# A fused attention-and-experts layer on one core: other orders of VectorE's and ScalarE's work per token tile

## The reference

```
x = L0_attn_x                                    # (2, 1024, 512) float32
sa, ca, ga, sb, cb, gb = the six parts of silu(c) @ wmod, per batch
h = layernorm(x) * (1 + ca) + sa
x = x + ga * mixer(h)
h = layernorm(x) * (1 + cb) + sb
x = x + gb * ffn(h)

mixer(h):  x_shift = (roll(h, -512) @ Wts.T) * g + h * (1 - g)
           xn = layernorm(x_shift) * ln_w + ln_b
           k, v = xn @ Wk.T, xn @ Wv.T
           wkv = exp(-exp(time_first) * sigmoid(k)) * v
           states = scan over the tokens: s = s * exp(time_decay) + wkv
           out = states @ Wo.T
ffn(h):    router softmax, the best 4 of 32 experts, at most 64 tokens per expert
           shared = silu(h @ Wsg) * (h @ Wsu) @ Wsd, times sigmoid(h @ Wse)
           each expert: silu(xe @ Wg) * (xe @ Wu) @ Wd, weighted, added to its tokens
```

## Time and profile before

| | us |
|---|---|
| median of 3 runs | 717.41 |
| lowest and highest run | 716.9, 723.52 |
| the profiled execution | 721.89 |
| its span | 720.1 |
| PE busy in the span | 675.2 (94%) |
| DVE, ACT, POOL busy | 365.6, 288.5, 184.7 |

### The profile page before, as it was taken

One profiled execution on the slowest core, in us unless ns is written; L12 is line 12 of the kernel. 1 busy time (PEld: TensorE's weight loads), 2 busy tenths in 40 slices (PEclk: granted clock), 3 DMA queues, 4 the chain that ended last, 5 costly groups with the idle time before them and its releaser, 6 DMA issues.

```text
span 720.1 us, 8883 instructions
## 1 busy us (share of the span) xinstructions
PE 675.2 (94%) x3218; PEld 470.2 (65%) x3218; DVE 365.6 (51%) x702; ACT 288.5 (40%) x552; POOL 184.7 (26%) x174
## 2 busy tenths in 40 slices
PE   4899699999998899998999899999999999999997
PEld 3666466777666667886665566666665666668875
DVE  3778677678688877763214223122121233225755
ACT  3435775565747623323225224233132343323231
POOL 1254474745536200001122022222221122120000
PEclk9789887999999999999999999999999999999999
DMA  7760200000241008107667767878899788816311
GB/s 272 269 216 0 76 15 30 15 30 30 74 145 60 15 1 313 53 1 268 239 237 237 256 218 248 265 237 282 271 317 325 242 270 266 285 21 235 115 50 70
DMA packets 50295, 118.27 MB, mean 164 GB/s; under 512 B 6904, under 2 KB 11084, under 8 KB 50252
## 3 DMA queue, kind: packets, MB, share of 16 engines
q1 hardware_dynamic: 45388, 109.31, 43.2%
q0 software_dynamic: 4864, 8.40, 5.4%
HBM read 100.87 MB, written 18.91 MB: 166 GB/s over the span
## 4 chain that ended last, share of the span: by engine, by line
PE 60%; DVE 6%; DMA 3%; ACT 3%; issue 2%; POOL 2%; SPq 0%; DVEq 0%; ACTq 0%; POOLq 0%
PE bank L1688 26%; PE bank L1700 11%; PE bank L1743 11%; PE bank L1760 6%; DMA egu<-in_L_ffn_Wu_dram 2%; PE bank L1731 1%; ACT xsH L863 1%; DMA xg<-h_rows,slot_tok 1%; PE bank L1791 1%; PE bank L1749 1%; DVE xres L1262 1%; POOL ho L637 1%; DVE prodL L1226 1%; DVE prod L1224 1%; POOL rsh L609 1%
## 5 line engine op out<-in xcount | busy, mean ns | idle before, releaser
L1688 PE MATMUL bank<-xsH,wguH 128*128 128x512 f32 x352 | 143.1, 406 | 1.1 <-DVE xsL L1216 0.7
L1688 PE MATMUL bank<-xsL,wguH 128*128 128x512 f32 x352 | 137.5, 391 | 0.0
L1688 PE MATMUL bank<-xsH,wguL 128*128 128x512 f32 x352 | 137.3, 390 | 0.0
L1743 PE MATMUL bank<-egu,xeT 128*64 128x352 f32 x512 | 81.0, 470 | 4.5 <-DMA egu<-in_L_ffn_Wu_dram 3.2
L1688 PEld LDWEIGHTS bank<-xsH,wguH 128*128 128x128 f32 x352 | 66.3, 188 | 25.0 <-issue 10.5
L1224 DVE TENSOR_TENSOR prod<-bank,silu 128x512 f32<-128x512 f32 x38 | 26.2, 690 | 110.3 <-PE bank L1688 87.7
L1700 PE MATMUL bank<-wdH,prodH 128*128 128x512 f32 x176 | 74.1, 421 | 6.3 <-DVE prodL L1226 4.2
L695 POOL DMA_INDIRECT expert_sums<-ye,slot_to x32 | 48.7, 1522 | 118.0 <-DMA expert_sums<-ye,slot_to 91.4
L1688 PEld LDWEIGHTS bank<-xsL,wguH 128*128 128x128 f32 x352 | 66.1, 188 | 14.6
L1688 PEld LDWEIGHTS bank<-xsH,wguL 128*128 128x128 f32 x352 | 66.3, 188 | 12.9 <-issue 0.7
L702 POOL DMA_INDIRECT xg<-h_rows,slot_tok x16 | 16.8, 1050 | 223.1 <-DVE slot_w L1370 89.9
(11 more groups left out here) (220 smaller groups left out, 1024.4 us busy)
## 6 DMA issues: line engine op xcount, KB each, us to landing
egu<-in_L_ffn_Wg_dram SPq DMA_DIRECT2D x32, 704.0 KB, 6.1
egu<-in_L_ffn_Wu_dram SPq DMA_DIRECT2D x32, 704.0 KB, 7.7
ed<-in_L_ffn_Wd_dram SPq DMA_DIRECT2D x32, 512.0 KB, 5.3
h2T<-in_L_wmod_dram SPq DMA_DIRECT2D x6, 1024.0 KB, 9.3
ed<-in_L_ffn_Wd_dram SPq DMA_DIRECT2D x32, 192.0 KB, 6.2
h_rows<-ho SPq DMA_DIRECT2D x16, 256.0 KB, 2.0
expert_sums<-ye SPq DMA_DIRECT2D x16, 256.0 KB, 8.6
out_dram<-xres SPq DMA_DIRECT2D x16, 256.0 KB, 2.2
```

Source lines behind the costliest of these rows:

```text
L1688: ins = mm.matmul(bk[:, :], l[f][:, w, c, :], r[:, c, :], start=(k == 0), stop=(k == 3 * C - 1))
L1743: ins = mm.matmul(bk[side, 0:F], xeT[:, c, side], egu[:, e, w, c, :], start=(c == 0), stop=(c == C - 1))
```

## The change

Three things are moved, and no operation is added or taken away. On ScalarE, all calls of `next_rows` stand ahead of `norm_mixed`, two of them in other steps than before, and `split_first` stands ahead of `norm_out`. On VectorE, `h_lo(t + 1)` stands behind `mix_front(t)` from step 5 on. And from step 6 on VectorE waits, before `scale_rows` and what follows it, until GpSimd has taken the power of tile t-5 (`rsh_ok`, raised by L609).

```
@@ ScalarE
                     if t in SPLIT_FIRST:
                         split_group(0, g + 1)
-                    for k in {7: (2,), 8: (4,), 9: (6,), 10: (7,)}.get(t, ()):
+                    for k in {5: (0,), 6: (1,), 7: (2,), 8: (3, 4), 9: (5, 6), 10: (7,)}.get(t, ()):
                         next_rows(ROWS[1][k])
                     if t < NT:
                         norm_mixed(t)
+                    if 4 <= t < 4 + NC0 + 1:
+                        split_first(t - 4)
                     if t in ROUTER_FIRST:
                         logits_out(router_group(t))
                     if 0 <= t - 5 < NT:
                         norm_out(t - 5)
                     if g >= 0 and s == 2:
                         exps(g)
-                    if 4 <= t < 4 + NC0 + 1:
-                        split_first(t - 4)
-                    for k in {5: (0,), 6: (1,), 7: (3,), 8: (5,)}.get(t, ()):
-                        next_rows(ROWS[1][k])
@@ VectorE
                     g, s = divmod(t - FFN_FROM, GT)
-                    if 1 < t + 1 < NT:
+                    if 0 < t <= GT:
                         h_lo(t + 1)
...
                     if t < NT:
                         mix_front(t)
+                    if GT < t and t + 1 < NT:
+                        h_lo(t + 1)
                     if 0 <= t - 5 < NT:
                         residual_sum(t - 5)
...
+                    if t >= 6:
+                        dve.wait_ge(rsh_ok, min(t - 4, NT))
                     if t >= 7:
                         scale_rows(t - 7)
```

More of the change, by code:

```diff
@@ L979, in _ @@
                         exps(g)
[L980 to L984, removed]
                     if scan_group(t) is not None:
```

## The result

The changed kernel takes 724.33 us (median of 4 runs, 723.76 to 726.39), the kernel before beside it 717.15 (716.12 to 723.52): a ratio of 1.0091, 95% interval 1.0057 to 1.0124, so 0.9% slower. The forecast was 724.9. The profiled execution took 726.39 us with a span of 724.6.

A forecast was written before the change was run, and what follows sets the result against it. TensorE is nearly always busy from 330 us on, so the end of the mixer's loop decides. Terms -1.2 + 2.0 + 1.0 + 2.0 + 3.7 = +7.5 us on the median 717.41 gave 724.9 us, range 708 to 731.

The forecast's parts named there:

- The sum of +7.5: Whole kernel: -1.2 + 2.0 + 1.0 + 2.0 + 3.7 = +7.5 us on the median, giving 724.9 us, 1.05% slower.
- ScalarE's side work and the early ring, -1.2: Step 7: hT about 2.2 us earlier, TensorE gains nothing there; of 0 to 2.2 reaching step 10, -1.2 us taken.
- The low part, +2.0, +1.0, +2.0: TensorE's turns of h2 wait for hT's low part: 2.0 us in step 10, 1.0 in 13, 2.0 in 14.
- The wait, +3.7: Scaling blocked by GpSimd's product, 1.8 us later each step; unhidden from step 17 on, 4.5 at most, 3.7 taken.
- a round of the ring: Steps 18 to 20: residual, power, output row, prodH, prodL, residual again; in steps 18 and 19 0.45 us longer each.
- what steps 6 to 16 were held to hide: Most of the scaling's 1.8 us, as VectorE idles there until hT or prodH; 1.8 a step if that cover is gone.
- the scaling isn't blocked: Rival: scaling costs 0.68 us behind the wait; +3.1 in all, 720.5 us, no difference; chance 0.25.
- The rival of the falling clock: Stalls of 2.0 us in steps 10 and 14 drop TensorE's clock to 1.2 GHz, 2 us each: 729 us; chance 0.10.
- The ring that opens early: Rival: TensorE better fed from 60 to 113 us, no turn stands if VectorE is ahead in step 10: 709.7 us; chance 0.20.
- the room that it was drawn from: From 60 to 113 us: 8.5 us of TensorE idling and 6.9 of half speed, half of it to be won.
- One of its signs: Signs for the early-opening ring: the granted clock from 60 to 120 us rises, and the loop ends early.

The follow-up runs named there:

- experiment 4: The kernel before with ScalarE's new order alone: 716.94 us, ratio 0.9959.
- Experiment 10: The kernel before with h_lo from step 5 on right behind the sum, ahead of its statistics: 720.36 us, ratio 1.0038.
- experiment 9: The kernel before with ScalarE's new order, and h_lo behind mix_front in steps 5 to 9 only: 715.83 us, ratio 0.9969.
- experiment 8: The kernel before with VectorE's wait alone, and GpSimd also waiting, behind its power, for VectorE's scaling: 718.17 us, ratio 1.0015.
- experiment 6: The changed kernel with VectorE's wait from step 17 on only: 726.05 us, ratio 1.0096.
- 11: The changed kernel with GpSimd also waiting, behind its power, for VectorE's scaling: 723.6 us, ratio 1.0072.
- 12: The kernel before with ScalarE's new order, VectorE's wait and GpSimd's wait for the scaling, low part in its old place: 717.08 us, ratio 0.9988.
- 7: The changed kernel with VectorE's wait in steps 6 to 16 only: 722.42 us, ratio 1.0052.
- 1: The changed kernel without VectorE's wait for the power: 720.78 us, ratio 1.0023.
- 3: The kernel before with h_lo behind mix_front from step 5 on, nothing else: 722.89 us, ratio 1.0072.

## Why the prediction came out right

**What bounds the kernel, and the sum.** The sum of +7.5 stands beside a timed +7.2 (+6.5 by the ratio). That they come so near is partly luck. In the profile the gain before step 10 was larger than forecast (-2.1 for -1.2), the low part's loss a little smaller (4.4 for 5.0) and the wait's tail near its price, which would leave the slots some 6 us late; a loss of 4.1 that was not in the sum takes that to 10.0, and some 3 of these don't show in the timed runs. The mechanisms of the two large terms, the stalls at the turns and the blocked scalings, are those that the runs show.

**ScalarE's side work and the early ring, -1.2.** Too small. hT of tile 8 starts 3.4 us earlier, not 2.2, in the changed kernel and in experiment 4, and the sum of step 10 is 2.1 earlier with all three parts, 3.4 with this one alone, which the time keeps (-2.9). The working priced step 7 only; in experiment 4 step 6 gave 1.6 as well (hT of tile 7 at 73.5, 76.3 before, less 1.1 of start). The changed kernel has that hT only 0.3 earlier, and the 1.6 at the sum of step 6. That TensorE would gain nothing in step 7 itself was right for the changed kernel, and is the low part's doing: with the old place its turn comes 6 us sooner.

**The low part, +2.0, +1.0, +2.0.** Right in place and size: 1.86, 0.67 and 1.73 us, and 4.4 us lost between step 10 and step 16 against a forecast of 5.0; alone it costs 5.2 in time. Experiment 10 shows that the loss goes with the length of the stalls, experiment 9 that longer ones ahead of step 10 cost next to nothing while VectorE doesn't wait for the power.

**The wait, +3.7.** The mechanism was right to the tenth: the scaling ends 4.31 us after the residual (forecast 214.2 less 209.88, 4.32), a round of the ring takes 0.35 more (forecast 0.45), step 17 1.5 (the residuals of steps 17 and 18 are 9.44 apart, 7.90 before), and from the last residual to the down piece it is 5.02 where it was 3.20, 1.8 more (forecast 1.8 each). That is 1.5 + 2 x 0.35 + 1.8 = 4.0. Short was what steps 6 to 16 were held to hide: with the low part late VectorE no longer idles for hT there (7.8 us between 60 and 113 us before, nothing after), and the wait takes some 1.6 us before step 10, as the working had it for a cover that is gone, without a price for these steps in the sum. The rival "the scaling isn't blocked" falls with the 1.75 us, and with experiment 8. The prediction gave it 0.25 since no scaling of before had come second. One had, in step 21, 0.86 us behind the start of a product of GpSimd: it took 0.98 us and ended 0.56 behind the product, as a blocked one would.

```profile
224.48 1.28 POOL L645 TENSOR_TENSOR xres<-xres,bc 128x512 f32<-128x512 f32 x1
225.34 0.98 DVE L1181 TENSOR_TENSOR ho<-ho,bc 128x512 f32<-128x512 f32 x1
```

**What was missed: the clock in step 20.** The rival of the falling clock was placed at the stalls of steps 10 and 14, where in the changed kernel's profile nothing of the kind happened; of the six profiles with a stall of 1.9 us in step 10 one, experiment 6's, has the fall behind it. In the changed kernel it came in step 20. TensorE waited 1.94 us for prodL, until 225.45, and at 226.1 the granted clock was down; the 1.65 us of waiting for the residual, until 230.33, lie within the slow stretch:

```profile
224.00:226.00 2.00, 0.55 (x2) 0.49 (x3) 1.30 (x3) 0.63 (x1) 0.75 (x1) 1.00 0.19 72
226.00:228.00 2.00, 2.00 (x8) 1.65 (x7) 1.24 (x5) 0.55 (x2) 0.72 (x2) 0.53 0.16 59
```

It made 5.5 us of delay into 9.6, 4.1 more. It comes in all four profiles with a blocked scaling in the tail and in none of the ten others, the kernel before (waits of 1.55 and 0.98 at the same places) and experiments 8, 11 and 12 (1.7 and 1.7) among them. With it the changed kernel's profile is 10.0 late at the slots.

**What gave some of it back.** Behind the slots that profile takes 458.63 us to its end, the kernel before's 463.33. From 300 to 430 us TensorE waits longer in the kernel before for the first experts' weights (`egu`), 3.2 us for 1.7. Behind that wait its clock falls, at 399 us, as it does at 337 us behind one of 2.3 for the experts' tokens (`xg`); in the changed kernel it stays at 1.00 throughout. The two falls cost 1.7 us of full clock each. With the 1.5 of waiting that is 4.9, about the difference of 4.7:

```profile
PE bank L1743 <- DMA egu<-in_L_ffn_Wu_dram: 3.2, 1, 3.2
```

```profile
300.00:430.00 130.00, 123.76 (x614) 84.12 (x613) 43.16 (x66) 38.81 (x73) 18.22 (x14) 0.97 0.58 196
```

It is no effect of the change that could be shown: in experiment 9, with its early loop, the wait is 1.7 too, and in experiment 10 it is 5.9. So the kernel before's profiled execution, 4.7 over the median of 717.15, is a long one for a reason behind the loop, and why the timed runs keep 6.5 to 7 of the loop's 10 us stays open.

**The ring that opens early** was half right: experiments 4 and 9, which leave the turns of h2 and the scaling alone, are 2.2 to 2.9 us faster than before, which makes them some 9 faster than the changed kernel. The 709.7 of that rival was not reached, and the room that it was drawn from had left out 3.0 us at the lower clock from 113 to 187 us (0.96 of 74 us): at the end of the loop their lead is 2.8 to 3.0 us. One of its signs did come: from 60 to 120 us the granted clock is 0.89 in the changed kernel and in experiments 4 and 9, and 0.83 before. In the changed kernel the loop ends late all the same, so a better clock early was no sign of an early end. Either of the two experiments is the version to keep.

## What to carry to other kernels

A wait that keeps one engine out of another's way decides who comes second, and so who is blocked: look at what the other engine has queued directly behind the instruction that is being protected. An instruction moved behind another is paid by whoever shares its buffer; it is free where that engine was waiting for something else anyway, and costs the whole stall where the engine had work. Price each part of a change with several parts by its own stretch, and price a stall of the matrix engine twice, once as idle time and once for the clock that may, but need not, fall behind it. A forecast that meets the time should still be added up again from the trace: here it met it with a loss missing and a gain too small.

## What the hardware showed beyond that

TensorE's clock fell to 0.50 after stalls that other executions went through at full clock. In experiments 6 and 7 it was down from 160 to 171 us behind the stall of 0.7 us in step 13, and cost 2.8 us by step 16, counted against the changed kernel; behind the same stall in the changed kernel and in experiments 1, 3 and 11 it stayed at 1.00. In experiment 6 it was down from 122.8 to 126.3 as well, behind the stall of 1.86 us in step 10, and cost 1.6; behind the same stall in the changed kernel and in experiments 1, 3, 7 and 11 it stayed at 1.00. Experiment 6:

```profile
118.00:124.00 6.00, 4.14 (x19) 3.11 (x18) 5.76 (x14) 1.24 (x3) 0.72 (x2) 0.90 0.12 44
124.00:130.00 6.00, 6.00 (x25) 4.83 (x24) 2.33 (x7) 5.17 (x11) 4.66 (x4) 0.81 0.01 1
...
160.00:166.00 6.00, 6.00 (x25) 5.49 (x25) 3.05 (x16) 2.16 (x5) 5.47 (x5) 0.53 0.00 0
166.00:172.00 6.00, 6.00 (x18) 4.23 (x16) 4.97 (x11) 4.12 (x8) 0.00 (x0) 0.62 0.13 46
```

A fall can also be free. In experiments 4 and 10 the clock was down for between 3 and 4 us in step 17, near 200 us, and between the residuals of steps 16 and 20 they lose nothing (0.02 and 0.00 us).

The wait for the first experts' weights, from 300 to 430 us, differs from execution to execution and makes much of their spread. TensorE's waits (us in total, times, longest) in the changed kernel and in experiment 10:

```profile
PE bank L1745 <- DMA egu<-in_L_ffn_Wu_dram: 1.7, 1, 1.7
```

```profile
PE bank L1745 <- DMA egu<-in_L_ffn_Wu_dram: 5.9, 1, 5.9
```

In that stretch the granted clock was 1.00 in the first and 0.96 in the second, and from the slots to the end they took 458.63 and 467.91 us. Over all fourteen profiles the four with waits of 3.9 to 5.9 us took 462.7 to 467.9 there, the four with waits of 1.7 to 1.9 took 456.7 to 460.4.
